# Twelve steps of lead instead of sixteen between maxima and exponentials in the rope and latent attention layers, and another order of their prologue and of SyncE's DMAs

## The reference, cut to what matters

```python
q = q * cos + rotate_half(q) * sin
k = k * cos + rotate_half(k) * sin
scores = jnp.einsum('bqhd,bkhd->bhqk', q, k) * scale
attn = jax.nn.softmax(scores, axis=-1)
out = jnp.einsum('bhqk,bkhd->bqhd', attn, v)
x = x + out.reshape(b, l, d) @ Wo
```

## Time and profile before

| | us |
|---|---|
| median of 3 runs | 2870.66 (2863.97 to 2878.41) |
| the profiled execution, its own time | 2863.06 |
| its span | 2861.3 |
| PE busy | 2315.3 (81%) |
| DVE busy | 1942.5 (68%) |
| ACT busy | 1535.4 (54%) |
| POOL busy | 911.8 (32%) |
| rope layer, from its first instruction to its last add | 899 to 1423 |
| latent layer, its first instruction | 2072 |

### The profile page before, as it was taken

The page is one execution under the profiler, slowest core; times in us unless marked ns, Lnnn a source line. Parts: engine busy times, 40 slices in busy tenths (PEclk is TensorE's granted clock), DMA queues, the critical chain, the costliest instruction groups (busy, mean ns, idle before and its releaser), DMA issues. The chain is left out here.

```text
span 2861.3 us, 40653 instructions
## 1 busy us (share of the span) xinstructions
PE 2315.3 (81%) x13550; PEld 1159.4 (41%) x13550; DVE 1942.5 (68%) x4549; ACT 1535.4 (54%) x2426; POOL 911.8 (32%) x851
## 2 busy tenths in 40 slices
PE   4799999999666799999757688389859999984698
PEld 2334444443453233333246455256522333323465
DVE  5788888887535888888462444577568888864343
ACT  2477676777623477777652333255427777772122
POOL 0232223330134244543024300435416545413211
PEclk7799999999887799999888899589959999996899
DMA  7565565651145121212016100556242121204242
GB/s 243 183 183 181 176 196 172 191 178 40 61 158 170 46 68 46 68 48 66 25 71 204 60 1 1 174 214 224 97 121 68 52 63 52 62 24 149 94 148 74
DMA packets 193506, 318.32 MB, mean 111 GB/s; under 512 B 29285, under 2 KB 155272, under 8 KB 188564
## 3 DMA queue, kind: packets, MB, share of 16 engines
q1 hardware_dynamic: 177764, 266.31, 29.8%
q0 software_dynamic: 15536, 49.41, 5.1%
HBM read 164.41 MB, written 151.59 MB: 110 GB/s over the span
## 5 line engine op out<-in xcount | busy, mean ns | idle before, releaser
L1816 DVE CUSTOM_DVE_ANT_0 decay_junk<-decay_scores_q,decay_corr 128x512 bf16<-128x512 f32 x512 | 338.3, 685 | 110.4 <-PE decay_scores_q L1553 108.7
L1733 ACT ACTIVATE decay_probs<-decay_scores_k 128x512 f32<-128x512 f32 x512 | 294.4, 597 | 189.3 <-PE decay_scores_k L1572 154.1
L2426 ACT ACTIVATE latent_probs<-latent_scores,latent_escale 128x1024 f32<-128x1024 f32 x256 | 281.8, 1115 | 137.0 <-PE latent_scores L2305 135.8
L2426 ACT ACTIVATE rope_probs<-rope_scores,rope_escale 128x1024 f32<-128x1024 f32 x256 | 282.6, 1115 | 133.3 <-PE rope_scores L2305 131.9
L2503 DVE TENSOR_REDUCE rope_mx<-rope_scores 128x2 f32<-128x1024 f32 x256 | 308.6, 1222 | 57.6 <-PE rope_scores L2292 56.1
L2503 DVE TENSOR_REDUCE latent_mx<-latent_scores 128x2 f32<-128x1024 f32 x256 | 307.9, 1221 | 53.3 <-PE latent_scores L2292 52.6
L1553 PE MATMUL decay_scores_q<-decay_KS,decay_QS 96*128 96x512 bf16 x512 | 204.2, 400 | 35.3 <-DVE decay_mx L1816 23.4
L1569 PE MATMUL decay_scores_k<-decay_QS,decay_KS 99*128 99x384 bf16 (+3 forms) x512 | 156.8, 307 | 14.9 <-DMA decay_QS<-decay_mT 7.2
L2318 PE MATMUL latent_out_heads<-latent_probs,latent_Vaug 128*32 128x512 f32 x1024 | 140.7, 622 | 6.7 <-ACT latent_Osb L2417 4.1
L2318 PE MATMUL rope_out_heads<-rope_probs,rope_Vaug 128*32 128x512 f32 x1024 | 138.1, 612 | 5.9 <-ACT rope_Osb L2417 4.1
L1597 PE MATMUL decay_out_heads<-decay_probs,decay_Vaug 128*32 128x512 f32 x1024 | 141.5, 626 | 0.8 <-DVE decay_probs L1828 0.8
(11 more groups left out here) (455 smaller groups left out, 5138.2 us busy)
## 6 DMA issues: line engine op xcount, KB each, us to landing
decay_KS<-decay_parts_dram SPq DMA_DIRECT2D x64, 384.0 KB
decay_QS<-decay_parts_dram SPq DMA_DIRECT2D x64, 384.0 KB
decay_parts_dram<-decay_parts SPq DMA_DIRECT2D x56, 384.0 KB, 3.1
experts3x_w<-in_w_dram SPq DMA_DIRECT2D x16, 1024.0 KB, 10.9
weight_parts<-experts3x_w SPq DMA_DIRECT2D x8, 2048.0 KB, 7.7
experts4x_w<-weight_parts SPq DMA_DIRECT2D x8, 2048.0 KB, 8.0
decay_parts_dram<-decay_parts SPq DMA_DIRECT2D x56, 256.0 KB, 3.3
experts_xin<-dispatched SPq DMA_DIRECT2D x96, 128.0 KB
```

The source lines that it names most:

```text
L1733: act.activation(probs[:, (b * 16 + kk) % PSLOTS, h, :], psB[:, s % 2, :], ACT.Exp, scale=scale).then_inc(exp_done, 1)
L1816: dve.tensor_tensor_reduce(junk[:, a % 2, :], psA[:, A_BANK[k], :], corr[:, qt, :], 1.0, -3.0e38, ALU.mult, ALU.max, mx[:, grp % 2, qt, h: ...
L2426: act.activation(probs[:, kk % 2, 2 * (u % 2):2 * (u % 2) + 2, :], psS[:, slot_of("exp", n), :, :], ACT.Exp, scale=escale[:, 0:1]).then_in ...
```

## The change

The lead of the maxima over the exponentials becomes LEAD = 12 steps in both layers, and the split of a group's maxima moves from steps 0, 8, 16, 24 of a batch to steps 4, 12, 20, 28. In the prologue, chains 2 and 3 of batch 0 move from VectorE and ScalarE to GpSimd, the first eight maxima come right after their two rotations, ahead of the remaining result adds and of batch 1's normalisation, and on TensorE v0, v1 and the transposes of batch 1 are spread among the first twelve maxima products. SyncE's list of DMAs is put in another order.

```diff
     late_rows, late_results = results.capacity, not results.capacity
-    STEPS, NM = 32, 8
+    STEPS, NM, LEAD = 32, 8, 12
     XN = 4 if project_q else 8
...
     NORMALISE_AT, PV_AT = 6, 1
+    V_BEHIND = [2, 5]
     TURNED_BY_DVE = ("OT", "Wo")
...
-        n = b * STEPS + u + 16
+        n = b * STEPS + u + LEAD
         return n if n < NB * STEPS else None
...
-    scores = [("top", n) for n in range(16)]
+    scores = [("top", n) for n in range(LEAD)]
     for n in range(NB * STEPS):
-        scores += [("exp", n)] + ([("top", n + 16)] if n + 16 < NB * STEPS else [])
+        scores += [("exp", n)] + ([("top", n + LEAD)] if n + LEAD < NB * STEPS else [])
     place = {x: i for i, x in enumerate(scores)}
...
                 eng.wait_ge(parts_written[j], 32 * nb)
-            copy = eng.copy if nb == 0 else eng.tensor_copy
+            copy = eng.copy if nb == 0 and j < 2 else eng.tensor_copy
             copy(parts[:, j, 0, :], fc[:, j % 2, :]).then_inc(high_done, 1)
...
-            for c in range(2):
-                for j in (2 * c, 2 * c + 1):
-                    write_parts(0, j)
-                load_half(0, c)
-            for grp in range(1):
-                write_rows(0, grp)
-                load_rows(0, grp)
+            for j in (0, 1):
+                write_parts(0, j)
+            load_half(0, 0)
+            for j in (2, 3):
+                write_parts(0, j)
+            write_rows(0, 0)
+            load_half(0, 1)
+            load_rows(0, 0)
...
                     write_parts(b + 1, 0)
+                    write_parts(b + 1, 1)
+                    load_half(b + 1, 0)
                 write_rows(b, 2)
-                if more:
-                    write_parts(b + 1, 1)
                 load_rows(b, 2)
                 if more:
-                    load_half(b + 1, 0)
+                    write_parts(b + 1, 2)
                 write_rows(b, 3)
+                if more:
+                    write_parts(b + 1, 3)
                 load_rows(b, 3)
                 if more:
-                    write_parts(b + 1, 2)
-                    write_parts(b + 1, 3)
+                    load_half(b + 1, 1)
                     write_rows(b + 1, 0)
-                    load_half(b + 1, 1)
                     load_rows(b + 1, 0)
...
             pe.matmul(psO[:, P:P + 2], ones2[:, :], diag[:, :], start=True, stop=True).then_inc(tops_spread, 1)
-            for name, nb in FIRST_USES[2:]:
-                if name in ("k0", "q0", "v0"):
+            for name, nb in FIRST_USES[2:-4]:
+                if name in ("k0", "q0"):
                     pe.wait_ge(loaded_by[f"w{name[0]}"], 16)
...
             pe.wait_ge(scales_ready, 1)
-            for n in range(16):
+            pe.wait_ge(loaded_by["wv"], 16)
+            for n in range(LEAD):
                 max_scores(n)
+                if n in V_BEHIND:
+                    work(f"v{V_BEHIND.index(n)}", 0)
+                if n == LEAD - 3:
+                    work("xT0", 1)
+                if n == LEAD - 1:
+                    work("xT1", 1)
             pe.wait_ge(ones_set, 2)
...
             for j, (o, c) in enumerate(CHAINS):
-                if ("kq"[o == "q"] + str(c), 0) in turn:
+                if (f"{o}{c}", 0) in turn:
                     take(f"{o}{c}", 0)
-                high_part(act, 0, j)
+                if j < 2:
+                    high_part(act, 0, j)
                 if pending:
...
             pending = list(range(FIRST, NB)) if late_results else []
-            for j in range(4):
+            for j in range(2):
                 rotate(0, j)
...
                 low_part(dve, 0, j)
-                if pending and j:
-                    results.add(dve, pending.pop(0), rst)
+            rotate(0, 2)
+            if pending:
+                results.add(dve, pending.pop(0), rst)
+            rotate(0, 3)
+            for n in range(NM):
+                maxima(n)
+            split_maxima(0, 0)
             while pending:
...
                 normalise(dve, 1, t)
-            for n in range(16):
+            for n in range(NM, LEAD):
                 maxima(n)
-                if n == 7:
-                    split_maxima(0, 0)
             if late_results:
...
                         maxima(top_of(b, u))
-                    if u % 8 == 0 and b * 4 + u // 8 + 1 < NB * 4:
+                    if u % 8 == 4 and b * 4 + u // 8 + 1 < NB * 4:
                         split_maxima(*divmod(b * 4 + u // 8 + 1, 4))
...
             pool.memset(Vaug[:, :, :, :, 16:32], 1.0).then_inc(ones_set, 1)
-            pool.wait_ge(loaded_by["xb" if biased else "tab"], 16)
+            pool.wait_ge(loaded_by["tab"], 16)
+            if biased:
+                pool.wait_ge(loaded_by["xb"], 16)
+            for j in (2, 3):
+                cosines(pool, 0, j)
+                rotary_sum(pool, 0, j)
+                high_part(pool, 0, j)
+                low_part(pool, 0, j)
...
```

## The result

| | before | changed |
|---|---|---|
| median of the runs, us | 2870.4 | 2932.9 (2915.6 to 2937.6, 4 runs) |
| ratio | 1 | 1.0205, interval 1.0155 to 1.0255 |
| profiled execution: span, us | 2861.3 | 2913.7 |

The changed kernel is 62 us slower; the forecast was 2933 us. The profiled execution is the fastest of its four runs, 52 us above that of before, and the trace is read against those 52.

What follows compares the result with a forecast made beforehand. TensorE was taken as the bound with little slack, so its waits add nearly in full. Starts -5.3, group 3's wait +49.0 and clock +18.7 give +62.4 on 2870.7: 2933 us, range 2895 to 2968.

Steps and rivals of the forecast that it cites:

- Group 3's wait, +49.0: Step 24: TensorE waits for rows loaded behind chain 3's parts, seven times 2.9 us in rope and 4.1 in latent.
- The clock, +18.7: After step 24's waits TensorE falls to its lower clock, 11 falls in 14 waits at 1.7 us each.
- Other parts: nothing: Splits moved to steps with a rotation or result add, and half loads with four more steps of slack, cost nothing.
- The prologue, -5.3: Layer starts: earlier maxima bring first exponentials 3.7 us (rope) and 4.6 us (latent) sooner, less 1.5 us a layer.
- The +1.5 us a layer at the end: Last steps that ran without maxima now have some: at most two pairs at 2.98 us instead of four exponentials at 1.115.
- Groups 0 and 1: Their row loads, now with four steps, cost nothing; upper bound 0.6 us for each of 28 loads.
- all rows late: Rival: row loads take as long as the write, groups 0 and 1 wait too, about 0.6 us each; 2953 us, chance 0.10.

Runs made afterwards that it cites:

- f2_swap_in_before: Kernel before (lead sixteen, old splits and prologue) with group 3's rows loaded behind chain 3's parts on SyncE; ratio 1.0281 to the kernel before.
- f3_busy_wait: Changed kernel with eleven unused matmuls on TensorE ahead of step 24's wait in batches 0 to 6; ratio 1.0201 to the kernel before.
- f1_rows_first: Changed kernel with one swap on SyncE, group 3's rows loaded ahead of chain 3's parts; ratio 1.0056 to the kernel before.
- g3_two_inputs: f1_rows_first with the split's first instruction written as a product of two SBUF tensors instead of tensor by constant; ratio 1.0081 to the kernel before.
- f4_prologue_only: Changed kernel's prologue alone, with lead of sixteen, splits and SyncE's batch order as in the kernel before; ratio 0.9955 to the kernel before.

## Why the prediction held, and which of its steps did not

- **Group 3's wait, +49.0: the mechanism right, the size too large.** The rows come 2.8 to 3.0 us after GpSimd's end (2.9 forecast; one latent batch 3.3), in seven batches of each layer. Idle time is 33.7 us, not 49.0. The step took TensorE to be at step 24 as early as before. It comes later, since step 22 had grown by itself, by about 0.9 us in rope and 1.8 in six of the latent batches, and what it has lost there it need not wait for again. f2_swap_in_before, where the splits stay, has the full waits: 57.7 us, with GpSimd's end 0.6 us later in each.
- **The clock, +18.7: measured 18.4.** Steps 24 and 25 took 5.5 to 6.7 us instead of 4.0 behind 10 of the 14 waits: 10 falls at 1.8, for 11 at 1.7. f3_busy_wait shows the share apart in rope.
- Wait and clock together were put at 67.7, and measured in the trace they are 52.1. Undoing the order gives back 43, to within about 15 (f1_rows_first); latent's step 14 and the clock there are worse in that run, which takes some of the gain.
- **"Other parts: nothing" is the step that failed.** It counted VectorE's instructions and found one split in steps 4 to 11 as before. It didn't ask what the split would run beside. Two of four splits moved into GpSimd's chains, where an instruction of 0.17 us takes 0.67 and 0.96, and TensorE has 2.0 us of slack a batch to hide this in. A rope batch is 2 us longer in f1_rows_first. The instruction's own longer time is 1.3 of them; the split beside a rotation at step 4 accounts for about half a microsecond more.
- **The prologue, -5.3: right in kind, too small.** The exponentials came 6.3 and 8.3 us sooner, for 3.7 and 4.6. In both the forecast ran v0 and v1 at half speed and only v0 did. From half 0's landing to the end of the eight maxima (941.25 in rope) it took 11.5 us in both, where I had 13.2 and 13.8; half 0 also landed 1.2 us sooner in latent. The +1.5 us a layer at the end did come: in the last batches steps 14, 15 and 17 together are 1.7 us longer in rope and 1.9 in latent. The totals (46.9 and 48.2 us, before 47.6 and 47.6) hide it, because rope's steps 27 to 29 are 2.9 us shorter (granted clock 1.00, before 0.51) and latent's 19 to 21 are 1.5 us shorter (1.00, before 0.68). No term of the forecast had this; it was luck.
- **Groups 0 and 1 cost next to nothing**, as said: apart from the 14 waits TensorE waited for rows eight times, 4.4 us in all, the longest 1.37 and 0.95 us at step 16 of the first batches. Nor does the longer way of the rival "all rows late" appear: with 0.6 us more, group 3's rows would have come 3.5 us after GpSimd's end. The section of the Trainium skill that the prediction quotes for it ("DMA: Bandwidth & Descriptors", Anatomy of one DMA) gives its 2.0 us for DMAs that GpSimd issues, and these are SyncE's.

So the parts are -14 for the starts, +43 for the order with the clock, and by what is left of the 62, some +30 for the rest, the splits' place above all. The first is read from the trace, the second was undone by itself. Of the third, the runs show the mechanism and its price in rope (2 us a batch, 14 in all) and not each us in latent, where the clock falls behind step 13 mix with it. The forecast of +62.4 had 67.7 in place of 43, nothing in place of the 30, and -5.3 in place of -14. That its total is right to a microsecond is luck. Two of these errors come from leaving the splits out and work against each other, since TensorE that loses time ahead of step 24 waits less at it; but nothing makes them equal. The sum was built on the profiled execution, and for that it gave 2925.5 us, 10 more than the 2915.6 of the changed kernel's.

## What to carry to other kernels

When a step moves, write down for each instruction what runs on the neighbouring engines in its new place, not only how full its own engine is. When the order of a DMA queue changes, look at which issue waits for an engine and what stands behind it; one line moved here was worth some 43 us, and the wait it made came with sixteen steps of lead as with twelve. And undo parts one at a time even when the total agrees with the forecast: one of the parts was a gain.

## What the runs showed of the hardware

**A short instruction of VectorE can wait for one of GpSimd's.** The clearest case is in latent of f1_rows_first:

```profile
2219.80 2.35 POOL L2622 TENSOR_TENSOR X<-X,latent_xb 128x1024 f32<-128x1024 f32 x1
2219.85 2.34 DVE L2521 TENSOR_SCALAR latent_mp<-latent_mx 128x16 f16<-128x16 f32 x1
...
2223.29 3.51 PE L2266 MATMUL latent_work<-latent_xnT,latent_wk 128*128 128x512 f32 x4 [2.30 <-DVE latent_attn L2535]
```

Sixteen elements a partition take 2.34 us and end 0.04 us after GpSimd's addition; TensorE idles 2.30 us for what follows, and its clock falls (3.51 us for four projections that take 1.98 at full speed). Not every instruction is held up: the maxima, which read PSUM, keep their 1.23 us beside GpSimd's products, and the transpose behind the split (L2529 of the changed kernel) takes its 0.21 us inside one. The Trainium skill has this ("SBUF — State Buffer", "SBUF: two separate sides"): GpSimd and VectorE share one pair of ports, held for a whole instruction, and a VectorE instruction is shut out if it is of a two-port form or has two inputs in SBUF (the latter only beside a GpSimd instruction that reads SBUF). g3_two_inputs agrees for the second form, 0.96 us. Whether the split's one-input instruction is of a two-port form, no run here shows.

**The same idle time doesn't always cost the clock.** In f3_busy_wait TensorE idled 1.20 us ahead of latent's step 22 in one batch and its clock fell (fillers at half speed); in the next it idled 1.21 us:

```profile
2385.93 0.66 PE L2274 MATMUL latent_work<-ident_sb,latent_attn 128*128 128x128 f32 x4 [1.21 <-DVE latent_attn L2540]
...
2388.60 2.54 PE L2305 MATMUL latent_scores<-latent_KS 48*128 48x512 f16 x11
```

and the eleven fillers ran in 2.54 us, full speed. The 2.09 us in rope's last batch are a second such pair: the value sums behind them took 1.94 us before and 1.06 in f4_prologue_only. What tells the two apart stays open.

**Chips differ** by more than most changes here: the kernel before took 2861, 2862 and 2803 us in the three sets of experiments, each on a chip of its own.
